# A weight conversion moved from the last phase of a fused layer into the attention loop, step by step

## The reference

```python
# attention: q, k, v projections with bias, rotary embedding on q and k, full softmax
scores = einsum('bhqd,bhkd->bhqk', q, k) / sqrt(64)
out = einsum('bhqk,bhkd->bhqd', softmax(scores), v)
x = layernorm(x + out)                      # no weights, eps 1e-5
# FFN: one 1024x1024 matmul on values rounded to float8_e4m3fn
ffn = quantize_e4m3(x) @ quantize_e4m3(weight).T + bias
x = layernorm(x + ffn)
```

## Time and profile before

| | us |
|---|---|
| three runs | 1282.34, 1282.42, 1313.47 |
| median | 1282.42 |
| the profiled execution, its own time | 1282.82 |
| its span on the slowest core (core 6) | 1281.3 |
| spans of the 8 cores | 1275.6 to 1281.3 |
| busy in the span: PE / DVE / ACT / POOL | 787.2 / 537.2 / 686.4 / 127.7 |

### The profile page before, as it was taken

How to read it: one execution, slowest core, us unless ns; L and a number is a source line. 1 busy time by engine, 2 the same in 40 slices (tenths; PEclk the granted TensorE clock), 3 DMA queues, 4 the chain that set the end, 5 groups by cost and what they waited for, 6 DMA issues and landing times.

```text
span 1281.3 us, 11529 instructions; the slowest of 8 cores (1275.6 to 1281.3 us)
## 1 busy us (share of the span) xinstructions
PE 787.2 (61%) x3560; PEld 297.6 (23%) x3584; DVE 537.2 (42%) x974; ACT 686.4 (54%) x729; POOL 127.7 (10%) x66
## 2 busy tenths in 40 slices
PE   0387756688877877877877878778720004443344
PEld 0333322233222222222222222222210001111111
DVE  4267857843012121121121121121144458888887
ACT  0000000001988888888888888888842335445542
POOL 0045745710000000000000000000000000000000
PEclk9897877889999999999999999999975556667777
DMA  9743152111700000000000000000000100000102
GB/s 140 110 66 66 33 99 66 34 33 38 241 1 1 1 1 1 1 1 1 1 1 1 1 1 1 1 0 1 1 33 33 50 16 1 33 33 33 50 33 82
DMA packets 15131, 42.79 MB, mean 33 GB/s; under 512 B 2144, under 2 KB 2272, under 8 KB 15072
## 3 DMA queue, kind: packets, MB, share of 16 engines
q0 software_dynamic: 6624, 15.73, 7.0%
q1 hardware_dynamic: 8448, 26.33, 6.9%
HBM read 36.81 MB, written 8.39 MB: 35 GB/s over the span
## 4 chain that ended last, share of the span: by engine, by line
ACT 29%; PE 28%; DVE 16%; issue 9%; DMA 8%; POOL 7%; SPq 3%; ACTq 0%; DVEq 0%; POOLq 0%
ACT PT L397 22%; PE ps L412 13%; PE ps_sc L384 9%; PE ps L283 4%; DMA srep_s<-srep 3%; POOL rs L248 2%; POOL rs L246 2%; POOL ro L249 2%; DMA wfs<-wfT 2%; DVE zf L687 1%; DMA wb<-wqT 1%; SPq L261 1%; DMA qT<-ro 1%; DVE zf L692 1%; PE ps L219 1%
## 5 line engine op out<-in xcount | busy, mean ns | idle before, releaser
L397 ACT ACTIVATE PT<-ps_sc,k_s 128x1024 bf16<-128x1024 f32 x512 | 543.0, 1111 | 78.8 <-PE ps L412 72.6
L412 PE MATMUL ps<-PT,va 128*65 128x512 bf16 x1024 | 318.8, 393 | 0.8 <-ACT PT L397 0.8
L384 PE MATMUL ps_sc<-qT,kT 64*128 64x512 bf16 x1024 | 201.3, 381 | 128.7 <-ACT PT L397 120.1
L451 DVE RECIPROCAL rc_sb<-ps 128x1 f32<-128x1 f32 x256 | 20.3, 151 | 369.0 <-PE ps L437 368.8
L397 ACT ACT_TABLE_LOAD x1 | 1.3, 1283 | 315.0 <-PE ps_sc L384 315.0
L219 PE MATMUL ps<-xT,wb 128*128 128x512 bf16 x501 | 126.5, 416 | 57.3 <-DVE qraw L230 48.3
L680 PE MATMUL ps<-wfq,yqT 128*128 128x512 bf16 x248 | 86.6, 519 | 118.4 <-ACT yqT L669 117.5
L384 PEld LDWEIGHTS ps_sc<-qT,kT 64*128 64x128 bf16 x1024 | 63.1, 93 | 312.6 <-issue 312.6
L427 DVE COPY oa_sb<-ps 65x1024 f32<-65x1024 f32 x32 | 39.1, 1221 | 145.2 <-PE ps L412 145.2
L412 PEld LDWEIGHTS ps<-PT,va 128*65 128x65 bf16 x1024 | 72.0, 110 | 117.5 <-issue 117.5
L219 PEld LDWEIGHTS ps<-xT,wb 128*128 128x128 bf16 x512 | 53.3, 105 | 130.2 <-issue 80.6
(11 more groups left out here) (74 smaller groups left out, 604.3 us busy)
## 6 DMA issues: line engine op xcount, KB each, us to landing
xf<-x SPq DMA_DIRECT2D x1, 8192.0 KB, 31.2
out<-xf SPq DMA_DIRECT2D x16, 512.0 KB, 2.6
xb<-x POOLq DMA_DIRECT2D x1, 4096.0 KB, 34.4
qT<-ro SPq DMA_DIRECT2D x32, 128.0 KB, 2.4
kT<-ro SPq DMA_DIRECT2D x32, 128.0 KB, 2.4
wfs<-wfT POOLq DMA_DIRECT2D x8, 512.0 KB, 3.5
wb<-wqT POOLq DMA_DIRECT2D x1, 2048.0 KB, 18.4
wb<-wkT POOLq DMA_DIRECT2D x1, 2048.0 KB, 17.2
```

The costliest lines, as they stand in the source:

```text
L384: return e.matmul(ps_sc[:, slot, half * 512:(half + 1) * 512], kT[r0:r0 + 64, hp, kt * 128:(kt + 1) * 128], qT[r0:r0 + 64, hp, q0:q0 + 512 ...
L397: return e.activation(PT[:, slot, :], ps_sc[:, slot, :], AF.Exp, bias=consts[:, C_SHIFT:C_SHIFT + 1], scale=0.125)
L412: return e.matmul(ps1[0:65, base:base + 512], va[:, kt, h * 65: h * 65 + 65], PT[:, slot, half * 512:(half + 1) * 512], start=(kt == 0), s ...
```

## The change

`emit_wf_chain` becomes `build_wf_steps`, which makes a list of 80 small functions: for each of the 8 chunks one for the load and one for each of the nine operations. Each of the operations is as before, except that it works in `qs_t` instead of `qs_w`. In the attention loop the list's next function is called at kt 4, 9 and 13 of every head from idx 4 on, behind `emit_exp(kt)` and ahead of that kt's copy, transpose or division. What is left of the list when the last phase begins is emitted there, ahead of round 0. `qs_w` is not allocated. Tile 0's use of `qs_t` waits for the end of the last conversion. The rounds call no chain any more.

```diff
-    def emit_wf_chain(cc):
-        ld_waits = list(bar2) if cc == 0 else [wf_toks[cc - 1]]
-        t_ld = DM("G", lambda e, cc=cc: e.dma_start(out=wfs[:], in_=wf3[:, cc, :]),
-                  waits=ld_waits)
-        tz = quant_chain(lambda: wfs[:],
-                         lambda cc=cc: wfq[:, cc, :],
-                         [t_ld] + ([wf_toks[cc - 1]] if cc else []), qs=qs_w)
-        wf_toks.append(tz)
+    wf_steps = []
+
+    def build_wf_steps():
+        state = {}
+        for cc in range(NC):
+            def s_ld(cc=cc):
+                ld_waits = list(bar2) if cc == 0 else [wf_toks[cc - 1]]
+                state["ld"] = DM("G", lambda e, cc=cc: e.dma_start(
+                    out=wfs[:], in_=wf3[:, cc, :]), waits=ld_waits)
+            def s_A(cc=cc):
+                state["A"] = A("S", lambda e: e.activation(
+                    qs_t[:, 0, :], wfs[:], AF.Abs, bias=0.0, scale=512.0),
+                    waits=[state["ld"]] + ([wf_toks[cc - 1]] if cc else []))
+            def s_L(cc=cc):
+                state["L"] = A("S", lambda e: e.activation(
+                    qs_t[:, 1, :], qs_t[:, 0, :], AF.Ln,
+                    bias=consts[:, C_025:C_025 + 1], scale=1.0),
+                    waits=[state["A"], t_k])
...
+            def s_Z(cc=cc):
+                tz = A("V", lambda e, cc=cc: e.tensor_scalar_mul(
+                    wfq[:, cc, :], qs_t[:, 2, :], 2.0 ** -9), waits=[state["Q"]])
+                wf_toks.append(tz)
+            wf_steps.extend([s_ld, s_A, s_L, s_M, s_E, s_S, s_Mt, s_P, s_Q, s_Z])
+
+    build_wf_steps()
@@ in the loop over heads, for kt in range(2, NT)
             emit_exp(kt, sc_tok)
+            if kt in (4, 9, 13) and wf_steps and idx >= 4:
+                wf_steps.pop(0)()
             if kt == 4 and post_q:
                 post_state[0] = post_evac(*post_q.pop(0))
@@ allocations of the last phase
-    qs_w, _qsw_cm = sb("qs_w", (128, 3, 1024))
@@ the loop of rounds
+    while wf_steps:
+        wf_steps.pop(0)()
+    rot_use["qs"][0] = wf_toks[-1]
     NSTG = 9
     for r in range(NT + NSTG - 1):
-        while len(wf_toks) < min(2 * (r + 1), NC):
-            emit_wf_chain(len(wf_toks))
         for stg in reversed(range(NSTG)):
```

More of the change, by code:

```diff
@@ L345, in build_nc, with s_M, s_E, s_S @@
     wf_toks = []
-    def emit_wf_chain(cc):
-        ld_waits = list(bar2) if cc == 0 else [wf_toks[cc - 1]]
-        t_ld = DM("G", lambda e, cc=cc: e.dma_start(out=wfs[:], in_=wf3[:, cc, :]),
-                  waits=ld_waits)
-        tz = quant_chain(lambda: wfs[:],
-                         lambda cc=cc: wfq[:, cc, :],
-                         [t_ld] + ([wf_toks[cc - 1]] if cc else []), qs=qs_w)
-        wf_toks.append(tz)
+    wf_steps = []
[15 more added lines that the diff above has]
+                    waits=[state["A"], t_k])
+            def s_M(cc=cc):
+                state["M"] = A("V", lambda e: e.tensor_scalar(
+                    qs_t[:, 0, :], qs_t[:, 1, :], consts[:, C_ILN2:C_ILN2 + 1],
+                    63.5, ALU.mult, ALU.add), waits=[state["L"], t_k])
+            def s_E(cc=cc):
+                state["E"] = A("V", lambda e: e.tensor_scalar(
+                    qs_t[:, 1, :], qs_t[:, 0, :], cder[:, 0:1], cder[:, 1:2],
+                    ALU.add, ALU.subtract), waits=[state["M"], t_C67])
+            def s_S(cc=cc):
+                state["S"] = A("S", lambda e: e.activation(
+                    qs_t[:, 0, :], qs_t[:, 1, :], AF.Exp, bias=0.0,
+                    scale=consts[:, C_LN2:C_LN2 + 1]), waits=[state["E"]])
+            def s_Mt(cc=cc):
+                state["Mt"] = A("V", lambda e: e.tensor_scalar(
+                    qs_t[:, 1, :], qs_t[:, 0, :], 1.0, cder[:, 0:1],
+                    ALU.max, ALU.mult), waits=[state["S"]])
+            def s_P(cc=cc):
+                state["P"] = A("V", lambda e: e.scalar_tensor_tensor(
+                    qs_t[:, 0, :], wfs[:], 512.0, qs_t[:, 1, :],
+                    ALU.mult, ALU.add), waits=[state["Mt"]])
+            def s_Q(cc=cc):
+                state["Q"] = A("V", lambda e: e.tensor_sub(
+                    qs_t[:, 2, :], qs_t[:, 0, :], qs_t[:, 1, :]), waits=[state["P"]])
+            def s_Z(cc=cc):
[3 more added lines that the diff above has]
+            wf_steps.extend([s_ld, s_A, s_L, s_M, s_E, s_S, s_Mt, s_P, s_Q, s_Z])
```

## The result

| | before | after |
|---|---|---|
| median of 8 runs, us | 1282.85 | 1212.64 (1212.0 to 1213.88) |
| ratio of the two, 95% interval | | 0.9456 (0.9445 to 0.9467) |
| profiled execution: time / span of the slowest core | 1282.82 / 1281.3 | 1212.14 / 1210.6 |
| spans of the 8 cores | 1275.6 to 1281.3 | 1204.0 to 1210.6 |

What follows compares the result with a forecast made beforehand. Attention was taken as bound by an exp, scores and PV loop sharing ACT, the last phase by DVE, with serial weight conversion between. 1282.8 - 98.7 + 19.9 = 1204 us, range 1194 to 1218.

Steps and rivals of the forecast that it cites:

- The last phase, -98.7 us: Between attention's last division and round 3, removing the serial weight conversion shrinks 105.1 us to 6.4.
- Rounds 3 and up unchanged: From round 3's first DVE step to the end, the time stays 232.6 us.
- DVE steps and loads at 0: In attention, the 48 DVE steps and 8 loads cost nothing; uncovered, DVE steps up to 48 x 1 us.
- ACT steps by place (0.67, 0.77, 0.95, 1.05): In attention, each ACT step costs 0.95 or 1.05 us behind kt 4, 0.67 or 0.77 behind kt 9 and 13.
- The sum of 19.9 us for attention: Total cost of the 24 ACT steps in attention: 8.2 at kt 4, 5.1 at kt 9, 6.6 at kt 13.
- rival (d): In heads 4 to 30 TensorE falls to its low clock level, giving about 1364 us; chance 0.02.
- Rival (b): In attention, steps cost up to 34 us through disturbed order or a held-up division, giving 1218 us; chance 0.12.
- (a): In attention, the ACT steps hide in ACT's 78.8 us of idle time, giving 1184 us; chance 0.06.
- (c): In attention, each lone Ln between Exps brings two table loads, 20.5 us, giving 1225 us; chance 0.02.
- (e): In the tail, the change gains nothing because something besides the chains holds the 105 us; 1302 us, chance 0.02.
- The sign of failure: A stretch of attention at granted clock 0.5, listed among observations that would show the forecast wrong.

Runs made afterwards that it cites:

- e1: The changed kernel with no conversion step in attention, all 80 emitted ahead of round 0; attention 627.9 us, profiled execution 1296.7 us.
- e6: The changed kernel with the weight conversion on DVE alone, an exponent mask replacing the ACT steps; median 1191.1 us, attention 627.8 us.
- e2: e1 plus one Abs on ACT behind the exp of kt 7 in each of heads 4 to 31; attention 646.6 us.
- e4: The changed kernel with steps at kt 5, 9, 13 instead of 4, 9, 13; median 1213.9 us, attention 652.4 us.
- e3: e1 plus one Abs on ACT behind the exp of kt 13 in each of heads 4 to 31; attention 667.5 us.
- e5: The changed kernel with steps at kt 3, 7, 11 instead of 4, 9, 13; median 1212.3 us, attention 645.2 us.

## Why the prediction was right, and where it was off

- **The last phase, -98.7 us: right.** 105.1 became 6.5. What made it easy is that both ends could be read off: all of the stretch was one serial chain, and what stays in it is a handful of operations with known durations. e1 shows the same from the other side.
- **Rounds 3 and up unchanged: right**, 233.3 against 232.6, and 232.1 in e1.
- **DVE steps and loads at 0: right**, as far as e6 shows it, with attention within 0.2 us of before for its 40 steps and 8 loads.
- **ACT steps by place (0.67, 0.77, 0.95, 1.05): right where the clock holds.** Heads 4, 7 and 10 to 12 meet it within 0.04 us, e2 gives 0.67 per Abs, e4 the 0.28 of the parted pair.
- **The sum of 19.9 us for attention: too small by 8.8 us** (mean of the cores; 9.9 on the slowest). The step that failed is the argument against rival (d). I read that PE idles 1.36 us at each head's start with the clock at 1.00, and took it as proof that such idleness does no harm. It only proved it for 1.36 us. My own steps at kt 13 delay the exp for which those scores wait, so the idle piece grows to 2.0 or 2.1 us, and the clock falls behind it at all nine such starts on the slowest core. I had put the fall of the clock into a rival in which it holds all through attention; it came for 3 to 4 us at a time and made 12 of 27 heads longer, by 0.5 to 1.3 us each.
- **Rival (b), steps cost more: true in size, not in cause.** The measured 1212.6 us is nearer to its 1218 than to my 1204. It named a disturbed order, which costs PE too, or a late division. The first describes the 2.1 us idle piece but not the fall of the clock, which is what costs; e6 gives nothing for a late division.
- **The range held in part by luck.** Its upper end, 1218, comes from rival (b), which has no term for the clock. Nine of 27 heads had an ACT step at kt 13. In e3, with one in each head, the fall cost 20.9 us; as an estimate, 1204 + 20.9 = 1225 us would have been outside.
- **Rivals (a), (c), (e): did not come.** The ACT steps do not hide; there is one table load; the last phase gave what it had.
- **The sign of failure** that I named, a stretch of attention at clock 0.5, is what the trace shows, for 3 to 4 us at a time.

## What to carry to other kernels

A step slid into a tight loop between two engines costs its length less the slack of that loop, and both come out of one period of the timeline; the idle time of ACT in the sum of the profile (here 78.8 us) said nothing about it. Beside ACT's time, look at what the step does to the longest idle piece of TensorE: put it far from the place where PE waits anyway, or take that wait away first. The cheapest place for such work is the engine that is idle, even if the arithmetic has to be written anew for it: the exponent mask took all 24 steps off ACT.

## What was not expected of the hardware

An idle piece 0.7 us longer can bring TensorE's clock down. With PE idle 1.36 us at each head's start the granted clock never fell at a start in the kernel before, e1, e2 and e6 (heads 5 to 31 of eight cores, 864 starts). With 2.0 to 2.1 us it fell to 1.2 GHz at 66 of 72 such starts in the changed kernel, 54 of 72 in e4 and 143 of 216 in e3. A fall lasted 3.4 us, sometimes twice that, and in it a kt takes 1.53 us instead of 1.15.

The length of that piece alone does not settle it. A third of the starts with the longer piece in e3 show no fall of their own. At the start of head 1, behind the low start of attention, the clock fell on 8 of the 32 cores of before, e1, e2 and e6 with a piece of 1.36 us. And at the start of head 9 in the changed kernel the clock fell with a piece of 1.35 us. PE's timeline there:

```profile
493.02 0.39 PE L424 MATMUL ps_sc<-qT,kT 64*128 64x512 bf16 x2 [0.63 <-ACT PT L437]
...
495.31 0.39 PE L424 MATMUL ps_sc<-qT,kT 64*128 64x512 bf16 x2 [1.35 <-ACT PT L437]
495.64 1.04 PE L452 MATMUL ps<-PT,va 128*65 128x512 bf16 x2
```

A second piece, of 0.63 us, stands 2.3 us earlier; together they are 1.98 us. The pairs of head 8 were parted by a step at kt 4. In the changed kernel 8 of the 144 starts with a last piece of 1.36 us show a fall, seven of them at idx 9, 19 and 29; in e4, where no pair is parted, none of 144 does. But six of the eight cores have both pieces at the start of head 9 and no fall, and e5 has a fall on two cores at idx 9 with no parted pair. What else counts, these runs do not tell apart.
